# Graph attention layer: mixing product turned around, leaky activation as a kept part plus a linear part

## The reference

```
def gat_layer(x, graph, W, b):
    h = x @ W
    s = einsum('bnd,bmd->bnm', h, h) * graph
    s = where(s == 0.0, NEG_INF, s)
    a = softmax(s, axis=2)
    return einsum('bnm,bmd->bnd', a, h) + b
heads = vmap(lambda W, b: gat_layer(x, graph, W, b))(Wh, bh)      # 8 heads
cat = heads side by side                                           # 8 * 128 channels
x = leaky_relu(cat, 0.01)
out = gat_layer(x, graph, W_out, b_out)
return leaky_relu(out, 0.01)
```

## Time and profile before

| | us |
|---|---|
| median of 3 runs (3857.81 to 3914.23) | 3859.68 |
| the profiled execution | 3857.22 |
| its span in the trace | 3855.4 |
| TensorE busy | 3626.9 |
| VectorE busy | 3017.7 |
| ScalarE busy | 2222.8 |
| GpSimd busy | 788.4 |

### The profile page before, as it was taken

The page is one execution under the profiler, slowest core; times in us unless marked ns, Lnnn a source line. Parts: engine busy times, 40 slices in busy tenths (PEclk is TensorE's granted clock), DMA queues, the critical chain, the costliest instruction groups (busy, mean ns, idle before and its releaser), DMA issues. The chain is left out here.

```text
span 3855.4 us, 59500 instructions
## 1 busy us (share of the span) xinstructions
PE 3626.9 (94%) x21435; PEld 2821.5 (73%) x21435; DVE 3017.7 (78%) x3715; ACT 2222.8 (58%) x3433; POOL 788.4 (20%) x507
## 2 busy tenths in 40 slices
PE   7996999999999999999999999979787999999976
PEld 3674988888888888888888888769654555555513
DVE  2577888888888888888888888678846999999825
ACT  0222666666666666666666666577534888888721
POOL 0221000000000000000000000000104889898711
PEclk9997999999999999999999999989898999999988
DMA  3000000000000000000000000000000000000000
GB/s 77 1 1 9 1 0 0 0 0 0 0 0 0 0 0 0 0 0 0 0 0 0 0 0 0 0 1 1 0 8 0 1 1 1 1 1 0 1 0 22
DMA packets 30174, 12.13 MB, mean 3 GB/s; under 512 B 27920, under 2 KB 29072, under 8 KB 30096
## 3 DMA queue, kind: packets, MB, share of 16 engines
q1 hardware_dynamic: 24864, 9.97, 1.1%
q10 hardware_dynamic: 5232, 1.12, 0.2%
HBM read 8.99 MB, written 2.10 MB: 3 GB/s over the span
## 5 line engine op out<-in xcount | busy, mean ns | idle before, releaser
L533 PE MATMUL hid_mix_ps<-X,hid_probsT 128*128 (+1 forms) x8192 | 975.0, 272 | 7.2 <-DVE hid_outs L597 7.2
L533 PEld LDWEIGHTS hid_mix_ps<-X,hid_probsT 128*128 128x128 f32 x8192 | 954.9, 192 | 14.4 <-issue 14.4
L544 DVE TENSOR_TENSOR hid_work<-hid_score_ps,A 128x1024 f32<-128x1024 f32 x512 | 626.3, 1223 | 360.3 <-PE hid_score_ps L505 359.2
L572 ACT ACTIVATE hid_work<-hid_work,hid_nmax 128x1024 f32<-128x1024 f32 x512 | 588.3, 1149 | 261.8 <-DVE hid_nmax L556 261.7
L1494 POOL TENSOR_TENSOR el<-el,node_edge 128x1024 f32<-128x1024 f32 x256 | 609.2, 2380 | 80.0 <-DVE el L1476 79.9
L556 DVE CUSTOM_DVE_ANT_0 hid_work<-hid_masks,hid_work 128x1024 f32<-128x1024 f32 x512 | 622.8, 1216 | 0.2 <-DVE hid_masks L564 0.2
L583 ACT COPY hid_probsT<-hid_turn_ps 128x512 f32<-128x512 f32 x1024 | 543.8, 584 | 68.3 <-PE hid_turn_ps L519 66.4
L519 PE MATMUL hid_turn_ps<-ident,hid_work 128*128 128x128 f32 x4096 | 530.7, 273 | 0.0
L519 PEld LDWEIGHTS hid_turn_ps<-ident,hid_work 128*128 128x128 f32 x4096 | 478.9, 140 | 69.3 <-issue 0.2
L1460 PE MATMUL summed<-el,window 128*128 128x512 f32 x1024 | 482.7, 594 | 4.4 <-DVE gT_acc L1482 3.6
L504 PE MATMUL hid_score_ps<-hid_SX,hid_Y 128*128 (+1 forms) x1024 | 478.1, 467 | 1.4 <-DVE hid_Yl L842 1.4
(11 more groups left out here) (269 smaller groups left out, 4090.3 us busy)
## 6 DMA issues: line engine op xcount, KB each, us to landing
A<-in_adj_dram SPq DMA_DIRECT2D x4, 1024.0 KB, 9.8
X<-in_x_dram SPq DMA_DIRECT2D x8, 256.0 KB, 8.5
out_dram<-X SPq DMA_DIRECT2D x8, 256.0 KB, 3.4
wa<-in_L_gnn_weight_dram ACTq DMA_DIRECT2D x2, 256.0 KB, 14.1
wb<-in_L_gnn_weight_dram ACTq DMA_DIRECT2D x2, 256.0 KB, 14.3
wh<-in_L_gnn_Wh_dram SPq DMA_DIRECT2D x2, 256.0 KB, 4.1
incid<-in_L_gnn_H_dram SPq DMA_DIRECT2D x2, 256.0 KB, 3.4
wo<-in_L_gnn_W_out_dram SPq DMA_DIRECT2D x1, 256.0 KB, 4.9
```

Of the source, the lines that this page charges most:

```text
L533: last_mm = nc.tensor.matmul(mix_ps[:, t * C:(t + 1) * C].unsqueeze(1), probsT[:, kk % 2, mt, :], value(ib, kk // NT, mt), start=(mt == 0) ...
L544: nc.vector.tensor_tensor(work[:, kk % 4, :], score_ps[kk % 2][:], A[:, kk % NT, :], ALU.mult).then_inc(s["weighted"], 1)
L572: nc.scalar.activation(work[:, kk % 4, :], work[:, kk % 4, :], ACT.Exp, bias=nmax[:, kk % 4:kk % 4 + 1], scale=-1.0, accum_out=rowsum[:, k ...
```

## The change

The mixing product is turned: x is the stationary operand (128x64, copied by GpSimd to `x_now`), and `probsT`, now laid out for groups of four tiles, moves, 512 columns in a product. Eight such products make a group; those of even mt go to partitions 0 to 63 of mix_ps, those of odd mt to 64 to 127, and the two partial sums are added by the next product, whose weight stands twice in `wh_now`. They are issued as two bursts of four, at odd steps. The result has nodes along the free axis, so the transposes T and their eviction go. The row sums' reciprocals must then lie along the free axis too: a use R of misc_ps turns them, broadcast, by four transposes, and ScalarE copies them to `rbc`; VectorE multiplies (four times of 512 columns in an item, two before) into Zn.

The leaky activation is written as 0.99 max(z, 0) + 0.01 z. ScalarE reads W with the bias through Relu into `kept`; the factor 0.99 is in `wo`; the linear part goes from Zn through the 64x64 matrix G = 0.01 Wh W_out of the head, and 0.01 b W_out is the start value `base` of h2T. VectorE's max is gone; O has four products in place of two. The uses of misc_ps stand in two tables: EARLY, made at the start of TensorE's step and read by ScalarE between exponential and eviction, and LATE, made at its end. G and base are made in the stage's set-up.

```diff
-            probsT = sb(f"{tag}_probsT", [P, 2, NT, P], F32, scope)
+            probsT = sb(f"{tag}_probsT", [P, 2, NT, group, P], F32, scope)
...
-                if not first or q >= 2:
-                    act.wait_ge(s["mixed"], q - 1)
+                if kk % group == 0 and (not first or q >= 2 * group):
+                    act.wait_ge(s["mixed"], BODY // group * i + (k - 3) // group - 1)
                 for half in range(2):
                     act.wait_ge(s["turned"], 2 * q + half + 1)
-                    nc.scalar.copy(probsT[:, kk % 2, half * 4:half * 4 + 4, :].rearrange("p a b -> p (a b)"),
-                                   turn_ps[half][:]).then_inc(s["copied"], 1)
+                    nc.scalar.copy(probsT[:, kk // group % 2, half * 4:half * 4 + 4, kk % group, :],
+                                   turn_ps[half][:].rearrange("p (a b) -> p a b", b=P)).then_inc(s["copied"], 1)
...
-            SMALL = {1: ("Y", 1, 0), 2: ("Y", 1, 1), 5: ("T", 0), 6: ("T", 1), 7: ("W", 0, 0), 8: ("W", 1, 0),
-                     9: ("W", 0, 1), 10: ("W", 1, 1), 11: ("Y", 0, 0), 12: ("Y", 0, 1), 13: ("O", 0), 14: ("O", 1)}
...
+            EARLY = {0: ("R", 8), 2: ("W", 14), 4: ("R", 8), 6: ("W", 14), 8: ("R", 8), 10: ("W", 14), 12: ("R", 8),
+                     14: ("W", 14)}
+            LATE = {2: ("Y", 1, 0), 4: ("Y", 1, 1), 8: ("O", 0), 10: ("Y", 0, 0), 12: ("O", 1), 14: ("Y", 0, 1)}
+            def group_of(i, k, lag):
+                d = (k - lag) // GROUP
+                return 4 * i + d, d % 4 // 2, d % 2, i + d // 4
...
+            def pe_early(pe, i, k, first, last):
+                if not present(k, False, first, last):
                     return
+                pe.wait_ge(misc_read, use(i, k, False, first, last))
+                g, u, half, ib = group_of(i, k, EARLY[k][1])
+                if EARLY[k][0] == "R":
+                    pe.wait_ge(s["inverted"], g + 1)
+                    pe.nop(nofuse=True)
+                    for a in range(GROUP):
+                        slot = u * NT + half * GROUP + a
+                        done = nc.tensor.transpose(misc_ps[:, a * P:(a + 1) * P],
+                                                   at.rinv[:, slot:slot + 1].to_broadcast([P, P]), ident[:])
+                else:
+                    if u == 0 and half == 0:
+                        pe.wait_ge(staged_w, ib + 1)
+                    pe.wait_ge(s["normed"], g + 1)
+                    pe.nop(nofuse=True)
+                    done = nc.tensor.matmul(misc_ps[:], wh_now[:], Zn[:, u, half, :], start=True, stop=True)
+                done.then_inc(misc_made, 1)
...
+            def pe_late(pe, i, k, first, last):
+                if not present(k, True, first, last):
+                    return
+                pe.wait_ge(misc_read, use(i, k, True, first, last))
+                if LATE[k][0] == "Y":
+                    _, u, half = LATE[k]
                     if u == 0 and half == 0:
                         pe.wait_ge(staged_m, i + 2)
                     b = 2 * (i // HEADS) + 1 if u else 2 * ((i + 1) // HEADS % J)
                     done = y_product(half, bass.ds(b, 1))
+                else:
+                    half = LATE[k][1]
+                    if half == 0:
+                        pe.wait_ge(staged_o, i)
+                    for u in range(2):
+                        nc.tensor.matmul(misc_ps[u * C:(u + 1) * C, :], wo_now[:], kept[:, u, half, :],
+                                         start=True, stop=False)
+                    for u in range(2):
+                        done = nc.tensor.matmul(misc_ps[u * C:(u + 1) * C, :], g_now[:], Zn[:, u, half, :],
+                                                start=False, stop=True)
+                done.then_inc(misc_made, 1)
+            def pe_burst(pe, i, k, first, last):
+                if k % 2 == 0 or (first and k < 7) or (last and k >= 7):
+                    return
+                part = (k - 7) % GROUP // 2
+                g, u, half, ib = group_of(i, k, 7)
+                if part == 0:
+                    pe.wait_ge(s["copied"], 2 * GROUP * (g + 1))
+                    if not first or g >= 1:
+                        pe.wait_ge(s["normed"], g)
+                    if half == 0:
+                        pe.wait_ge(staged_x, 2 * ib + u + 1)
                     pe.nop(nofuse=True)
+                for mt in range(4 * part, 4 * part + 4):
+                    rows = slice(mt % 2 * C, (mt % 2 + 1) * C)
+                    done = nc.tensor.matmul(mix_ps[rows, :], x_now[:, u, mt, :],
+                                            at.probsT[:, half, mt].rearrange("p t q -> p (t q)"),
+                                            start=(mt < 2), stop=(mt >= NT - 2))
+                if part == 1:
+                    done.then_inc(s["mixed"], 1)
+            def act_early(act, i, k, first, last):
+                if not present(k, False, first, last):
+                    return
+                n = use(i, k, False, first, last)
+                g, u, half, _ = group_of(i, k, EARLY[k][1])
+                act.wait_ge(misc_made, n + 1)
+                if EARLY[k][0] == "R":
+                    if not first or g >= 1:
+                        act.wait_ge(s["normed"], g)
+                        act.nop(nofuse=True)
+                    nc.scalar.copy(rbc[:], misc_ps[:]).then_inc(misc_read, 1)
                 else:
+                    nc.scalar.activation(kept[:, u, half, :], misc_ps[:], ACT.Relu,
+                                         bias=bh_now[:]).then_inc(misc_read, 1)
+            def act_late(act, i, k, first, last):
+                if not present(k, True, first, last) or LATE[k][0] != "Y":
                     return
+                _, u, half = LATE[k]
+                act.wait_ge(misc_made, use(i, k, True, first, last) + 1)
...
+            def vec_late(vec, i, k, first, last):
+                if not present(k, True, first, last):
+                    return
+                if LATE[k][0] == "Y":
+                    _, u, half = LATE[k]
+                    cols = slice(half * HALF, (half + 1) * HALF)
+                    vec.wait_ge(y_hi, 2 + 4 * i + Y_ORDER.index(k) + 1)
+                    nc.vector.tensor_tensor(Yl[:, u, cols], misc_ps[:], Y2[:, u, cols], ALU.subtract).then_inc(misc_read, 1)
                 else:
+                    half = LATE[k][1]
+                    acc = h2T[:, bass.ds((i - 1) // HEADS, 1), half * HALF:(half + 1) * HALF]
+                    vec.wait_ge(misc_made, use(i, k, True, first, last) + 1)
+                    nc.vector.tensor_tensor(acc, acc, misc_ps[:].unsqueeze(1), ALU.add).then_inc(misc_read, 1)
+            def vec_invert(vec, i, k, first, last):
+                if k % GROUP != 2 or (first and k < 6) or (last and k >= 6):
                     return
+                g, u, half, _ = group_of(i, k, 6)
+                slots = slice(u * NT + half * GROUP, u * NT + (half + 1) * GROUP)
+                vec.wait_ge(s["exped"], GROUP * (g + 1))
+                nc.vector.reciprocal(at.rinv[:, slots], at.rowsum[:, slots]).then_inc(s["inverted"], 1)
+            def vec_norm(vec, i, k, first, last):
+                if k % GROUP != 2 or (first and k < 10) or (last and k >= 10):
+                    return
+                g, u, half, _ = group_of(i, k, 10)
+                vec.wait_ge(s["mixed"], g + 1)
+                vec.wait_ge(misc_read, use(i, k - 2, False, first, last) + 1)
+                vec.nop(nofuse=True)
+                nc.vector.tensor_tensor(Zn[:, u, half, :], mix_ps[:], rbc[:], ALU.mult).then_inc(s["normed"], 1)
 
...
             def pe_step(pe, i, k, first=False, last=False):
+                pe_early(pe, i, k, first, last)
                 at.pe_scores(pe, i, k, first, last, wait_y, lambda ib, u: bass.ds(2 * (ib // HEADS) + u, 1))
                 at.pe_turn(pe, i, k, first, last)
-                at.pe_mix(pe, i, k, first, last,
-                          lambda ib, u, mt: Xrows[:, bass.ds(ib // HEADS * (2 * NT) + 2 * mt + u, 1), :])
-                pe_small(pe, i, k, first, last)
+                pe_burst(pe, i, k, first, last)
+                pe_late(pe, i, k, first, last)
 
             def act_step(act, i, k, first=False, last=False):
+                if k:
+                    act_late(act, i, k - 1, first, last)
                 at.act_exp(act, i, k, first, last)
+                act_early(act, i, k, first, last)
                 at.act_copy(act, i, k, first, last)
-                act_small(act, i, k, first, last)
 
             def vec_step(vec, i, k, first=False, last=False):
                 at.vec_weigh(vec, i, k, first, last)
+                vec_norm(vec, i, k, first, last)
                 if k:
-                    vec_small(vec, i, k - 1, first, last)
+                    vec_late(vec, i, k - 1, first, last)
                 at.vec_shift(vec, i, k, first, last)
                 at.vec_zero(vec, i, k, first, last)
```

(58 more changed lines are left out.)

123 lines of the change are left out of this document (44 added, 79 removed).

## The result

The change makes the kernel faster: the ratio to the kernel before is 0.950 (95% interval 0.934 to 0.965), and 0.952 (0.950 to 0.954) when the changed kernel was run again. The profiled execution took 3673.7 us in place of 3857.2, with a span of 3671.8; the medians of four runs are 3699.8 us after and 3887.0 before.

The account below looks back on a forecast made before the run. TensorE was taken to bound the stage: its item falls from 66.3 to 57.3 us, plus 3.7 of waits 61.0. 5.3 x 32 = 170, and 3 once, give 3684 us profiled, 3687 median; range 3570 to 3800.

Parts of the forecast that it names:

- signs that it named: Profile after: burst span 1.9 us, TensorE idle about 6% of the stage, VectorE busy 88%, item 61 us.
- a sum of parts: TensorE's item in the changed stage: scores, transposes, bursts and misc_ps uses add to 57.3 us, 9.0 less.
- O's row: Trace row: O's two products into two partition halves span 1.08 us, like W's one; hence a burst of 2.01.
- Rivals 2 and 3: Mixing bursts: passes start only in program order, 3780 us, chance 0.14; halves don't overlap in a chain, 4129, chance 0.07.
- Rival 2: Bursts and O: passes start only in program order, each costing 0.43 us more; 3780 us, chance 0.14.
- (a): TensorE before R at k = 4, 12, 0: VectorE, late, reads Y behind its weigh; 0.54 us each, 1.6 together.
- (b): TensorE before LATE in steps 4, 8, 12: ScalarE reads EARLY behind the exponential; 0.53, 0.99, 0.54 us, 2.1 together.
- VectorE at 53.9 us, ScalarE at 42: Busy time in one item of the changed stage: VectorE from 54.8 to 53.9 us, ScalarE from 41.0 to 42.
- GpSimd's copies to x_now, 0.8 us, at no cost: GpSimd copies 512 columns twice, 0.8 us each: nothing, or 51 us if VectorE were held up outright.
- Once only, -3: Outside the repeated items: set-up plus 7 us, the stage's end some 10 us less, net -3.
- rival 1: Changed stage without any wait: TensorE's own sum holds, 288 us less, so 3569 us; chance 0.13.

Follow-up runs that it names:

- both orders turned: Changed kernel, with ScalarE reading EARLY before its exponential and VectorE reading LATE before it weighs; 3546.5 us, ratio 0.920 when run again.
- full-width run: Changed kernel with a 128-column stationary operand into all 128 partitions, so no two products run side by side; other sums computed; 3945.6 us.
- eight products in one visit: Changed kernel with all eight mixing products of a group at steps 1, 5, 9, 13 and none at 3, 7, 11, 15; 3914.3 us.

## Why the prediction was right

It gave 3684 us for the profiled execution, which took 3673.7, and 3687 for the median of the runs, which was 3699.8. The sum is to be held against the first: 0.3 us less in each of 32 items is what lies between them. The signs that it named came: TensorE is idle in 5.9% of the stage (6% stated), VectorE busy in 88% (88%), a burst spans 1.94 us (1.9). Step by step:

- *TensorE is the stage's bound, its busy time a sum of parts.* Right. Its own sum after was put at 57.3; 60.7 less 3.6 of waits is 57.1, and with both orders turned the whole item is 56.6.
- *The burst costs 2.01, from O's row.* Right. From scores to scores, the odd step at 1539.33 takes 4.24 us; without R (0.40) and without scores and transposes (1.80, the step from 1515.96 to 1517.77) the burst is 2.04. The full-width run shows what it would be otherwise, 3.43. Rivals 2 and 3 are out.
- *Rival 2, passes in strict order.* The Trainium skill (TensorE: Matmul & The Clock Gate, The mechanism) has matmuls start and end strictly in order. No record here names the product that a pass belongs to, but with even, even, odd, odd in the program the passes still start in pairs 0.43 us apart and the burst keeps its length of 1.94 us; strict order would have made it 3.3 us, as worked out before that run. The measurement decides.
- *The waits, 1.6 us from (a) and 2.1 from (b), item 61.0.* Right in kind, place and size: 1.85 and 1.74, at the uses named, item 60.7. The prediction had the wait before O at step 8 as the longest, 0.99; the longest measured is 0.91. Each of the two causes was then taken away by an order of two lines, and the waits went with it.
- *VectorE at 53.9 us, ScalarE at 42.* 53.0 and 41.9 measured.
- *GpSimd's copies to x_now, 0.8 us, at no cost.* The price was too low and made no difference: a mean of 1.13 us, but no wait in the trace names them, and a weighing takes VectorE 1216 ns (1223 before).
- *Once only, -3.* Measured -1.3: set-up +3.5 where I had +7 (the 32 instructions for `base` took 1.88 us, not 4.5 to 7), the end, from the last first score to the next stage's load, 33.5 to 28.7 us, 4.8 less, where I had 10. Two misses that cancel, which is luck. At the end O's first use stands before the last W, so the chain is W, O, W, O and not one W and one O.

Where the trace would have allowed more: the sum of TensorE without waits stood in the prediction as rival 1, 3569. Both orders turned give 3546, with 56.6 for the item. That rival was no mishap to be weighed against the forecast but the next change to make.

## What to carry to other kernels

When a product's output has 64 rows, look for a place in the trace where two such products go to the two halves of the partitions: whether they run side by side is read from one row, and here it decided whether turning the product pays at all (item 60.7 or 67.4, for 66.3 before). After a bound engine has been relieved, walk one period with the slots of all engines: here it gave size and place of the new waits to a few tenths of a microsecond, and with them the two edits of order that bring another 127 us, beside the 184 of the change. Try such edits together as well as alone; a wait that only moves looks like an edit that does nothing.

## What the runs showed of the hardware

A burst of four products with 64 output rows, two for each half of the array, took 1.94 us in either program order, and its passes started in pairs. So the two halves seem to keep their own order of loads and passes. I had expected loads to go in program order.

GpSimd's copy of 128x512 to x_now took 0.61 us in the set-up and 1.13 us in the mean inside the stage. The runs show beside which instruction: where VectorE's zero mask (L564) never falls into the copy, at full width and with eight products in one visit, every copy took 0.61 to 0.62 us (the first row below, of the full width); in the changed kernel the mask does fall into it. With both orders turned one copy in each item starts beside the shift and meets the mask, and then both are stretched, the copy to 1.68 us and the mask from 0.69 to 1.10:

```profile
L858 POOL COPY x_now<-X x65: 610/616/618, 333.3 to 2511.9; 128x512 f32 x62, 128x512 f32<-128x512 f32 x3
```

```profile
555.26 1.68 POOL L858 COPY x_now<-X 128x512 f32 x1 [25.90 <-PE hid_mix_ps L749]
...
556.38 1.10 DVE L564 TENSOR_SCALAR hid_masks<-hid_work 128x1024 f32<-128x1024 f32 x1
```

So such a copy isn't always free for VectorE: there it costs 0.4 us an item. A copy in the set-up beside another instruction of VectorE (L929, which reads PSUM) took 0.61 us. What the mask and the shift have that L929 hasn't was not tested.
